# Two expert stages of a 16-stage network: every expert over every token, or each token's row sent to the tiles of its two experts

## The reference, cut to what matters

```
n    = layernorm(x)
lg   = n @ gate_w + gate_b                       # 8 experts
mask = 1 for the two experts with the largest lg
y_e  = relu(n @ w1[e] + b1[e]) @ w2[e] + b2[e]   # 128 -> 512 -> 128
x    = x + sum over e of mask[e] * y_e
```

## Time and profile before

| | |
|---|---|
| median of 3 runs | 3075.86 us (3069.61 to 3077.2) |
| the profiled execution | 3070.64 us, of which the trace spans 3069.1 us |
| TensorE busy, of the span | 82% |
| VectorE, ScalarE, GpSimd busy | 55%, 48%, 26% |
| mean granted TensorE clock | 0.931 of full speed |

### The profile page before, as it was taken

How to read it: one execution, slowest core, us unless ns; L and a number is a source line. 1 busy time by engine, 2 the same in 40 slices (tenths; PEclk the granted TensorE clock), 3 DMA queues, 4 the chain that set the end, 5 groups by cost and what they waited for, 6 DMA issues and landing times. The chain is left out here.

```text
span 3069.1 us, 34392 instructions
## 1 busy us (share of the span) xinstructions
PE 2515.8 (82%) x11930; PEld 1073.7 (35%) x11930; DVE 1690.9 (55%) x2653; ACT 1485.2 (48%) x2500; POOL 787.1 (26%) x740
## 2 busy tenths in 40 slices
PE   6678789999598799767766787899995988997677
PEld 2222335444343243223222223354543432432232
DVE  5958465555413611895569583655554136118855
ACT  5535546555343544545455264465552435445454
POOL 3730240002013312551047202400020133126510
PEclk8998999999798899999989898999997988999999
DMA  2011000000011110000000110000000111100000
GB/s 113 0 31 53 7 9 1 1 1 1 14 42 31 53 55 0 1 1 1 14 2 0 32 52 7 9 1 1 1 1 14 41 31 53 55 0 0 1 1 14
DMA packets 37382, 57.33 MB, mean 19 GB/s; under 512 B 7760, under 2 KB 20048, under 8 KB 37072
## 3 DMA queue, kind: packets, MB, share of 16 engines
q1 hardware_dynamic: 32848, 51.10, 5.2%
q10 hardware_dynamic: 4352, 3.94, 0.5%
HBM read 41.12 MB, written 13.63 MB: 18 GB/s over the span
## 5 line engine op out<-in xcount | busy, mean ns | idle before, releaser
L2042 ACT ACTIVATE L1b_pr<-ps,L1b_mneg 128x512 f32<-128x512 f32 x256 | 173.8, 684 | 190.9 <-DVE L1b_mneg L2083 190.9
L2081 DVE TENSOR_REDUCE L1b_m<-ps 128x2 f32<-128x1024 f32 x128 | 156.8, 1225 | 88.6 <-PE ps L1932 82.8
L1293 POOL TENSOR_TENSOR L0a_db<-L0a_du,L0a_bs 128x1024 f32<-128x1024 f32 x64 | 150.5, 2361 | 105.8 <-DVE L0a_du L1404 60.2
L1293 POOL TENSOR_TENSOR L3a_db<-L3a_du,L3a_bs 128x1024 f32<-128x1024 f32 x64 | 150.4, 2360 | 105.5 <-DVE L3a_du L1404 60.9
L1716 ACT ACTIVATE L0b_pt<-ps 128x1024 f32<-128x1024 f32 x128 | 125.7, 1023 | 97.8 <-PE ps L1616 97.7
L91 ACT ACT_TABLE_LOAD x44 | 56.5, 1283 | 239.3 <-PEq L1034 40.8
L1804 DVE TENSOR_REDUCE L0b_mx<-ps 128x1 f32<-128x512 f32 x256 | 157.9, 684 | 20.8 <-PE ps L1603 18.2
L2107 DVE COPY L1b_prt<-ps 128x512 f32<-128x512 f32 x128 | 88.5, 692 | 126.3 <-PE ps L1945 126.0
L1421 DVE TENSOR_TENSOR_SCAN L0a_hs<-ps,L0a_db 128x1024 f32<-128x1024 f32 x64 | 146.1, 2282 | 4.6 <-ACT ps L1213 4.6
L1421 DVE TENSOR_TENSOR_SCAN L3a_hs<-ps,L3a_db 128x1024 f32<-128x1024 f32 x64 | 146.1, 2282 | 3.8 <-ACT ps L1213 3.8
L260 POOL CAST L1g_xc<-xn 128x512 bf16<-128x512 f32 x2 | 1.5, 732 | 558.3 <-DVE xn L137 558.3
(11 more groups left out here) (600 smaller groups left out, 5593.8 us busy)
## 6 DMA issues: line engine op xcount, KB each, us to landing
L2f_w<-expert_dram SPq DMA_DIRECT2D x32, 256.0 KB, 3.0
L2g_w<-expert_dram SPq DMA_DIRECT2D x32, 256.0 KB, 3.0
L0b_qs<-stack_dram SPq DMA_DIRECT2D x32, 96.0 KB, 2.2
stack_dram<-L0b_cut SPq DMA_DIRECT2D x24, 128.0 KB, 2.1
L2b_qs<-stack_dram SPq DMA_DIRECT2D x32, 96.0 KB, 2.2
stack_dram<-L2b_cut SPq DMA_DIRECT2D x24, 128.0 KB, 2.1
weights<-w_dram SPq DMA_DIRECT2D x3, 936.0 KB, 15.3
weights<-w_dram SPq DMA_DIRECT2D x3, 935.5 KB, 13.6
```

What stands on the lines that cost most here:

```text
L1293: pool.tensor_tensor(db[:, n % DEEP, :, :], du[:, b, :, :], bcast(bs[:, n % DEEP, :], 1, 2), ALU.mult).then_inc(input_ready, 1)
L2042: act.activation(pr[:, s % 2, h, :], g.ps[:, 2 * (s % 2) + h, :], ACT.Exp, bias=mneg[:, s % 2, h:h + 1], accum_out=total[:, u % 2, t, h:h ...
L2081: dve.tensor_reduce(m[:, s % 2, :], g.ps[:, 2 * (s % 2):2 * (s % 2) + 2, :], AX.X, ALU.max).then_inc(max_raw, 1)
```

## The change

Each token is worked on only by its two experts. The stage now has these parts.

1. **Plan.** TensorE turns `xn` to rows of tokens (and ScalarE writes them twice to `tok`, 144 numbers wide: 128 features, then the token's number). From the mask two groups of small products count the tokens of each expert and rank each token within its expert; VectorE works out for each of the 2,048 (token, expert) pairs a row number `slot`, so that each expert's rows begin at a multiple of 128. At most 23 tiles of 128 rows come out (`SLOTS` = 23), and all 23 are always computed.
2. **Send.** GpSimd issues 16 indirect transfers, each of which scatters 128 rows of `tok` to the rows `slot` of a DRAM buffer. SyncE waits for all of them and loads the 23 tiles back in 6 groups of up to four.
3. **Tiles.** For each tile TensorE turns the rows back (by groups), does four 128x128x128 products for the hidden layer and four for the result. ScalarE reads the tile's expert number into a register and copies that expert's 1,028 columns of weights and biases from `wall` to one of three buffers `wsel`. VectorE does the four relus and copies the result out. GpSimd scatters the 128 result rows by one indirect transfer for each tile.
4. **Add.** When all 23 have come back, SyncE loads the rows by token, VectorE adds the two rows of each token, TensorE turns them back onto the bias term, and VectorE adds them to `xs`.

The core of the diff:

```diff
             def _(sp):
                 st.clear_spent(sp)
                 for e in range(E):
-                    sp.dma_start(w1[:, e, :], g.experts[0, :, e * FF:(e + 1) * FF]).then_inc(expert_in, 16)
-                    sp.dma_start(w2[:, e, :], g.experts[1, :, e * FF:(e + 1) * FF]).then_inc(expert_in, 16)
-                    sp.wait_ge(expert_in, 32 * (e + 1))
+                    sp.dma_start(wall[:, e, 0:FF], g.experts[0, :, e * FF:(e + 1) * FF]).then_inc(expert_in, 16)
+                    sp.dma_start(wall[:, e, FF:2 * FF], g.experts[1, :, e * FF:(e + 1) * FF]).then_inc(expert_in, 16)
+                sp.wait_ge(sent, 16 * 2 * NT)
+                for k in range(groups):
+                    a, z = GROUP * k * P, (GROUP * k + size(k)) * P
+                    sp.dma_start(xg[:, GROUP * k:GROUP * k + size(k), :], g.slots[a:z, :].rearrange("(t p) w -> p t w", p=P)).then_inc(group_in[k], 16)
+                sp.wait_ge(returned, 16 * SLOTS)
+                for b in range(NB):
+                    rows = g.rows[2 * b * T:2 * (b + 1) * T, :].rearrange("(t p k) c -> p t k c", p=P, k=2)
+                    sp.dma_start(back[:, b * KT:(b + 1) * KT, :, :], rows).then_inc(back_in[b], 16)
...
                 def hidden_products(n):
-                    b, e = n // E, n % E
-                    if b == 0:
-                        pe.wait_ge(expert_in, 32 * (e + 1))
+                    pe.wait_ge(chosen, n + 1)
+                    if n % GROUP == 0:
+                        pe.wait_ge(x_in, n // GROUP + 1)
+                    if n >= 2:
+                        pe.wait_ge(relu, n - 1)
                     for f in range(FT):
-                        if n >= 1:
-                            pe.wait_ge(relu, (n - 1) * FT + f + 1)
-                        elif f == 0:
-                            pe.wait_ge(picks, 1)
-                        pe.matmul(g.ps[:, f, :], w1[:, e, f * P:(f + 1) * P], g.xn[:, b, :], start=True, stop=True).then_inc(hidden, 1)
+                        mm = pe.matmul(g.ps[:, n % 2, f * P:(f + 1) * P], wsel[:, n % 3, f * P:(f + 1) * P],
+                                       xt[:, n // GROUP % 2, n % GROUP, :], start=True, stop=True)
+                    mm.then_inc(hidden, 1)
 
                 def results(n):
-                    e = n % E
+                    pe.wait_ge(relu, n + 1)
                     if n >= 2:
-                        pe.wait_ge(masked, n - 1)
+                        pe.wait_ge(y_in, n - 1)
                     for f in range(FT):
-                        pe.wait_ge(relu, n * FT + f + 1)
-                        mm = pe.matmul(g.ps[:, 6 + n % 2, :], w2[:, e, f * P:(f + 1) * P], h[:, n % 2, f, :],
+                        mm = pe.matmul(g.ps[:, 2 + n % 2, 0:P], h[:, n % 2, f, :], wsel[:, n % 3, FF + f * P:FF + (f + 1) * P],
                                        start=(f == 0), stop=(f == FT - 1))
                     mm.then_inc(out_ready, 1)
...
+                def choose(n):
+                    if n >= 3:
+                        act.wait_ge(out_ready, n - 2)
+                    e = act.value_load(expert_of[0:1, n:n + 1], min_val=0, max_val=E - 1)
+                    act.activation(wsel[:, n % 3, :], wall.rearrange("p e c -> p (e c)")[:, bass.ds(e * SET, SET)], ACT.Copy).then_inc(chosen, 1)
...
+                pool.wait_ge(slots_ready, 1)
+                for b in range(NB):
+                    pool.wait_ge(tok_in, 2 * b + 2)
+                    for t in range(b * KT, (b + 1) * KT):
+                        for k in range(2):
+                            pool.indirect_dma_start(g.slots[:, :], bass.IndirectOffsetOnAxis(ap=slot[:, k * NT + t:k * NT + t + 1], axis=0),
+                                                    tok[:, k, t, :], None).then_inc(sent, 16)
+                for n in range(SLOTS):
+                    pool.wait_ge(rows_ready, n // GROUP + 1)
+                    pool.wait_ge(y_in, n + 1)
+                    pool.indirect_dma_start(g.rows[:, :], bass.IndirectOffsetOnAxis(ap=row[:, n:n + 1], axis=0),
+                                            y[:, n, :], None).then_inc(returned, 16)
+                pool.wait_ge(sent, 16 * 2 * NT)
+                pool.wait_ge(returned, 16 * SLOTS)
+                pool.dma_reset()
```

More of the change, by code:

```diff
@@ L434, in expert_ffn @@
         hit = st.sb("hit", [P, NT, E])
[L435 to L436 removed]
+        picks_of = st.sb("picks_of", [P, 2, NT, E])
         top = st.sb("top", [P, NT, 1])
         mask = st.sb("mask", [P, NT, E], BF16)
[L439 to L443 removed]
@@ L444, in expert_ffn @@
[L444 to L448, removed]
+        below = st.sb("below", [P, P], BF16)
+        ones = st.sb("ones", [P, E])
+        count = st.sb("count", [P, E])
+        over = st.sb("over", [P, E, E])
+        tiles_of = st.sb("tiles_of", [P, E])
+        end = st.sb("end", [P, E])
@@ L488, in results @@
                                        start=(f == 0), stop=(f == FT - 1))
                     mm.then_inc(out_ready, 1)
+                turn(0)
                 hidden_products(0)
[L492 to L502, removed]
+                for n in range(SLOTS):
+                    if n % GROUP == 0 and n // GROUP + 1 < groups:
+                        turn(n // GROUP + 1)
+                    if n + 1 < SLOTS:
@@ L508, in _ @@
                 ln.scalar(act)
[L510 to L523, removed]
+                for b in range(NB):
+                    act.wait_ge(tok_turned, b + 1)
+                    act.wait_ge(cleared, 1)
+                    for k in range(2):
+                        act.activation(tok[:, k, b * KT:(b + 1) * KT, 0:P], g.ps[:, 6 + b, :].rearrange("p (t c) -> p t c", c=P), ACT.Copy).then_inc(tok_in, 1)
@@ L525, in _ @@
+                choose(1)
+                x_copy(0)
+                for n in range(SLOTS):
+                    if n + 2 < SLOTS:
+                        choose(n + 2)
+                    if n % GROUP == 0 and n // GROUP + 1 < groups:
+                        x_copy(n // GROUP + 1)
             @block.vector
@@ L531, in _ @@
                 k = 1
-                for pick in (first, second):
+                for c in range(2):
+                    pick = picks_of[:, c, :, :]
                     dve.wait_ge(picks, k)
@@ L547, in _ @@
[L547 to L550, removed]
-                    dve.wait_ge(out_ready, n + 1)
[L552 to L556, removed]
+                    if c == 0:
+                        dve.scalar_tensor_tensor(out=lg[:, :, :], in0=pick, scalar=NEG, in1=lg[:, :, :],
+                                                 op0=ALU.mult, op1=ALU.add).then_inc(picks, 1)
+                        k += 6
@@ L558, in _ @@
+                for b in range(NB):
+                    dve.wait_ge(total, b + 1)
+                    dve.tensor_tensor(g.xs[:, b, :], g.xs[:, b, :], g.ps[:, 6 + b, :], ALU.add).then_inc(added, 1)
             @block.gpsimd
             def _(pool):
[L560 to L566, removed]
+                pool.memset(tok.rearrange("p k t w -> p (k t) w")[:, :, P:WIDE], 0.0).then_inc(cleared, 1)
```

189 lines of the change are left out of this document (185 added, 4 removed).

## The result

The changed kernel takes **2967.32 us** (median; 2965.19 to 2970.57) where the kernel before takes 3072.74 in the same session (3066.89 to 3077.2): a ratio of 0.9659, with a 95% interval of 0.9638 to 0.968. It is 105 us faster; 41.6 were forecast.

A forecast was written before the change was run, and what follows sets the result against it. TensorE alone was taken to bound the expert stages' 16 steps. Seven parts summed to 120.1 us against 130.5 for L2f, 10.4 less; four stages save 41.6, giving 3034 us, range 2945 to 3130.

The forecast's parts named there:

- signs of being wrong: Scatters at 2 us or under 1, a tile over 2.8 or under 2.1, or other stages changing over 2.
- The second sign: Outside the four expert stages: the forecast is wrong if any other stage changes by over 2 us.
- Parts 1, 2, 4, 7: In stage L2f: until the mask 14.0 us, plan 3.0, loading the tiles back 3.4, way back 12.8.
- part 7: End of L2f, the way back: last scatter, loads, sums, turning, last addition and barrier, 12.8 us.
- Part 3: In L2f, 16 scatters on GpSimd one behind the other, 1.35 us each, and the last landing 2.2: 23.8 us.
- The rival in which GpSimd's issue decides: Exposed scatters and last return: saving gone at 1.96 us each; 3078 us at 2.0, 3103 at 2.36; chance 0.19.
- The rule weighed there: GpSimd's queue: some 2.0 us per transfer whatever its size; if paid one after another, 44 us higher, 3078.
- Part 6: In L2f, 23 tiles at ScalarE's 2.33 us each, 53.6, plus 4.0 for tiles at half clock: 57.6 us.
- Part 5: In L2f, filling the pipeline with TensorE at half clock: turning, copy, hidden layer, relus and hops, 5.5 us.
- Cheaper: Expert stages: scatter 0.8 us, register read beside ScalarE's copy, TensorE's 2.0 us sets the tile: 2966 us; chance 0.28.
- The register read is a trip: ScalarE in the tiles: the read takes 2.0 us, a tile 3.5; 110 us more, 3144; chance 0.10.
- The clock stays low: Tiles: TensorE may not get full speed and needs 4.0 us a tile; 138 us more, 3172; chance 0.05.

## Why the prediction was right in kind and wrong in size

**What bounds the kernel and which stages change**: right. The change lies in the four stages, 25.8 us each in the mean. Two of the signs of being wrong came up: a tile takes 1.91 us, under 2.1, and two untouched stages moved by over 2 us, L1a and L2b of the second pass, by 4.0 and 2.05. The second sign was set too narrow, since untouched stages move as much between the traces of the experiments.

**Parts 1, 2, 4, 7**: right, each within 0.5 us. The hops and plain loads came from rows of the same kind. In part 7 the nearness is in part luck. The sum had 1.5 us for the second load and 1.7 for turning half of the sums behind it; the trace has TensorE turning all eight tiles without a pause, 16 instructions at half clock, 3.56 us.

**Part 3, the scatter** (1.35 us, the middle of 0.33 and 2.36, so its nearness is partly luck): 1.26 measured, and the last landed 1.35 us after its end for 2.2. The part is 2.3 us too dear, 9 us in the four stages. The rival in which GpSimd's issue decides needed 1.96 us and is refuted. The rule weighed there (the Trainium skill, DMA: Bandwidth & Descriptors, Anatomy of one DMA: a fixed part of some 2.0 us for each transfer of GpSimd's queue, whatever its size) agrees with the one transfer that is seen to its end: from the last issue's start to SyncE's issue behind it are 879.34 - 877.03 = 2.31 us. But the 2 us were paid once and not 16 times.

**Part 6, the tiles, is the step that failed.** The prediction put ScalarE's hop, register read, register instructions, copy, second hop and share of the group copy in a row, 2.33 us, and let it set the tile. Its durations were nearly right: hop, read and registers 0.82 for 1.05, copy 1.06 for 1.03; that is 0.20 of the miss. Wrong was that they add up at each tile. A chain of waits that spans several buffers is a loop, and a loop has to be divided by the tiles that it spans. Here it takes 3.82 us for two tiles, and in a pair with a turning TensorE's own need, 4.02, is the larger. So the tile is 1.91, 0.42 less; times 22 intervals 9.2 us a stage. With the measured durations the row of steps would still give 0.82 + 1.06 + 0.1 + 0.15 = 2.13. The plainest proof is the run with half of the result products: its tile, 1.646, is shorter than hop, read, registers and copy of one tile, 1.88. The experiment with a second copy shows the same from the other side: ScalarE as a row of dependent steps would have given 2.33 + 1.03 = 3.4 us a tile, and it gave 2.34. "Three buffers let ScalarE run ahead" stood in the prediction, as an argument against a rival, and was not applied to the forecast itself.

**Part 5 and the clock** are the rest, some 5 us a stage. Eight instructions were counted to turn a group where the trace has four: a product stands there as two, but a turning of a tile of the group (L549) as one. The clock was priced twice over, in the fill (1.7 and 1.7 us) and by 4.0 more in part 6: of L2f's tiles only the first hidden products ran wholly at half clock (2.05 us for 0.9), the second in part. With full clock the fill is 4.98 us for 6.9 to 8.0, so the low clock costs 2 to 3 us in it, where the prediction had 5.6 (0.8 of the turning, 0.8 of the products, 4.0).

**The sum of the corrections**: parts 1, 4 and 7 give 0.42 + 0.34 + 0.45, part 2 takes 0.45, part 3 gives 2.3, parts 5 and 6 give 13.9: 17.0 us, and 120.1 - 17.0 = 103.1. Four times 17.0 is 68, and 3034 lies 67 us above the measured time.

**The rivals.** *Cheaper* named 2966 us, which is nearly the time, by half of its mechanism: TensorE nearly sets the tile, but no scatter costs 0.8, and the read stands behind its wait and not beside a copy. It had 9.4 us a stage from the scatters, which gave 2.3, and 7.6 from the tiles, which gave 13.9 with the fill; that the two errors cancel is luck. *The register read is a trip*: no, 0.6 us; it does lie in the loop, and a second read costs 20.8 us in the four stages. *The clock stays low*: no, 1.00 in the tiles from 892.4 on.

## What to carry to other kernels

When a change makes a chain between engines, write down which buffer each wait is for and how many tiles the chain spans, and compare the chain divided by that number with each engine's own need; adding its steps up for every tile overstates it. A register read that depends on nothing late belongs ahead of the wait for the buffer, where it cost nothing: the tile is 1.847 with the read there as without any read. What has to go through DRAM by row is paid by the instruction (1.26 us for each on GpSimd, on the path), and TensorE, which has little to do meanwhile, comes out of it at 1.2 GHz. Spare products kept the clock up through the whole fill only where they ended within 0.9 us of the work itself. And read a change of a few microseconds from the stages that it touches, since the others move by as much between two executions.

## What the runs showed of the hardware that was not expected

- An indirect transfer of GpSimd costs 1.20 us for 64 rows of 144 numbers and 1.26 for 128, 0.30 of it between two instructions.
- ScalarE's register read with its check takes 0.63 us behind a wait that has just been met (0.53 with the register instructions, by the copy's start when it was moved), and nothing beside a running copy: copies then follow at 0.95 us, closer than the 1.06 that one is shown to last.
- After 3.63 us without work TensorE was granted 1.2 GHz again. After 4.0 to 4.1 us, in three stages of the same run, and after 1.55 us in another run it began at full clock and fell during the light work that followed. After 0.3 to 0.9 us it kept 2.4 GHz through the whole fill, in seven stages of seven. Whether the pause or the light work behind it decided there is open: both were there, and no run parts them.
- A busy share of 99% at full clock hid a loss of 3%: the tiles show 38.67 of 39.00 us busy with 8.6 instructions in a microsecond, and with the read moved 39.17 of 39.50 with 8.8. The spacing of equal instructions told it, the busy time of the products didn't. That of the weight loads (PEld) did: 37.60 of 39.00 us against 38.98 of 39.50.
